# One copy of ScalarE moved ahead of two squares, and the centring of an image's first channels moved from VectorE to GpSimd

## The reference, cut to what matters

```python
x = x + dct2(group_norm(x))            # x is (16, 32, 112, 112), a 2-D cosine transform of each channel
y = group_norm(x)
for k in range(6):                     # six Euler steps of an ODE
    h = relu(gn1(y)); h = conv3x3(h, w1, t=k/6) + b1
    h = relu(gn2(h)); h = conv3x3(h, w2, t=k/6) + b2
    y = y + gn3(h) / 6
return x + y
```

## Time and the profile before

| | |
|---|---|
| median of 3 runs | 3459.21 us (3457.57 to 3469.12) |
| the profiled execution, its own time | 3467.75 us |
| span of its profile | 3465.9 us |
| mean granted TensorE clock | 0.935 |
| busy: PE / DVE / ACT / POOL | 3005.5 / 2717.9 / 2440.3 / 875.2 us |

### The profile page before, as it was taken

One profiled execution on the slowest core, in us unless ns is written; L12 is line 12 of the kernel. 1 busy time (PEld: TensorE's weight loads), 2 busy tenths in 40 slices (PEclk: granted clock), 3 DMA queues, 4 the chain that ended last, 5 costly groups with the idle time before them and its releaser, 6 DMA issues.

```text
span 3465.9 us, 148163 instructions
## 1 busy us (share of the span) xinstructions
PE 3005.5 (87%) x61684; PEld 2541.5 (73%) x61684; DVE 2717.9 (78%) x6273; ACT 2440.3 (70%) x3819; POOL 875.2 (25%) x1293
## 2 busy tenths in 40 slices
PE   3699988999889998899988999899988999888984
PEld 2578776777777787678767877777777777777873
DVE  6688876888868887788877888688886888768883
ACT  0377777677776777777776777777777767787774
POOL 3134311432123221223212331133311332111111
PEclk8799998999999999899999999999998999999997
DMA  3400033112231330322304213221133113131014
GB/s 84 89 22 22 25 55 96 49 49 80 37 96 49 91 72 4 96 77 69 68 18 112 66 49 68 59 87 49 50 67 96 49 49 92 25 95 59 31 49 112
DMA packets 370208, 217.56 MB, mean 63 GB/s; under 512 B 354544, under 2 KB 354912, under 8 KB 367456
## 3 DMA queue, kind: packets, MB, share of 16 engines
q1 hardware_dynamic: 369504, 207.64, 24.2%
HBM read 104.85 MB, written 77.07 MB: 52 GB/s over the span
## 4 chain that ended last, share of the span: by engine, by line
ACT 23%; PE 23%; issue 20%; DVE 20%; POOL 6%; DMA 3%; SPq 3%; DVEq 1%; POOLq 0%; ACTq 0%
PE cps L1482 16%; ACT z L714 8%; ACT z L682 6%; DVE y L1118 3%; PE sps L1597 3%; POOL m L562 3%; ACT unread_z L702 3%; PE tps L1588 3%; SPq L449 2%; DVE ha L1114 2%; DVE bnt L1144 2%; ACT hb L713 2%; ACT ha L713 2%; DVE hb L1114 2%; DMA y<-xa 2%
## 5 line engine op out<-in xcount | busy, mean ns | idle before, releaser
L1482 PE MATMUL cps<-ha,w 64*64 64x392 f16 (+1 forms) x27648 | 1418.8, 347 | 126.3 <-ACT z L682 75.4
L1482 PEld LDWEIGHTS cps<-ha,w 64*64 64x64 f16 x27648 | 1081.1, 110 | 332.0 <-issue 159.0
L1482 PE MATMUL cps<-hb,w 64*64 64x392 f16 x27648 | 1278.5, 334 | 20.8 <-issue 14.1
L1482 PEld LDWEIGHTS cps<-hb,w 64*64 64x64 f16 x27648 | 1091.7, 108 | 114.3 <-issue 25.9
L682 ACT ACTIVATE z<-cps,bias_now 128x784 f32<-128x784 f32 (+2 forms) x1056 | 759.1, 737 | 582.3 <-PE cps L1482 578.4
L519 POOL TENSOR_TENSOR small<-small,half 128x1 f32<-128x1 f32 x304 | 168.1, 553 | 1646.0 <-DVE small L1018 1008.4
L1114 DVE TENSOR_TENSOR ha<-z,ha 128x784 f16<-128x784 f32 (+2 forms) x384 | 385.0, 1003 | 150.4 <-ACT z L714 145.6
L1114 DVE TENSOR_TENSOR hb<-z,hb 128x784 f16<-128x784 f32 (+2 forms) x384 | 374.8, 976 | 86.6 <-ACT z L714 77.8
L1144 DVE BATCH_NORM_STATS2 bnt<-z 128x6 f32<-128x392 f32 (+1 forms) x768 | 385.8, 547 | 56.1 <-ACT z L682 55.7
L1118 DVE SCALAR_TENSOR_TENSOR y<-z,small,y 128x784 f32<-128x784 f32 (+2 forms) x384 | 396.4, 1035 | 0.1
L714 ACT ACTIVATE z<-z,small 128x784 f32<-128x784 f32 (+2 forms) x384 | 396.1, 1031 | 0.0
(11 more groups left out here) (161 smaller groups left out, 2650.9 us busy)
## 6 DMA issues: line engine op xcount, KB each, us to landing
xa<-x_dram SPq DMA_DIRECT2D x128, 196.0 KB, 5.1
y<-xa SPq DMA_DIRECT2D x16, 1568.0 KB, 7.6
y_dram<-y SPq DMA_DIRECT2D x128, 196.0 KB, 4.7
x_dram<-x1s SPq DMA_DIRECT2D x30, 784.0 KB, 6.0
fin<-y_dram SPq DMA_DIRECT2D x30, 784.0 KB, 7.5
xs<-in_x_dram SPq DMA_DIRECT2D x116, 196.0 KB, 4.5
fin<-x_dram SPq DMA_DIRECT2D x28, 784.0 KB, 5.7
out_dram<-fin SPq DMA_DIRECT2D x28, 784.0 KB, 3.6
```

The costliest lines, as they stand in the source:

```text
L1482: return pe.matmul(dst, w[hin * 64:(hin + 1) * 64, kx, a, wl, :], src[:, :, 0:NA], start=(what == "X" and n == 0), stop=(what == "Y" and n ...
```

## The change

On ACT the copy of batch 0 moves from behind the squares 2 and 3 of the second image, and behind the last part of the first image's new state, to a place ahead of the two squares. Centring of batch 0 leaves DVE and goes to GpSimd; GpSimd now centres batches 0 and 1 ahead of the first image's seam, and batch 2 behind it.

```diff
@@ GpSimd, normalise(n, b)
                 for c in range(4 * b, 4 * b + 4):
                     last = nc.gpsimd.tensor_scalar(xn[:, c, :], xs[:, c, :], m0[:, 4, c:c + 1],
                                                    m0[:, 6, CQ + c:CQ + c + 1], ALU.mult, ALU.add)
+                if b == 0:
+                    last.then_inc(xn_first, 1)
+                    pool.wait_ge(xn_first, n - HALVES + 1)
+                    return
                 last.then_inc(xn_done, 1)
@@ GpSimd, step
                 if kind == MID:
+                    normalise(HALVES * (g + 1) + s, 0)
                     normalise(HALVES * (g + 1) + s, 1)
+                seam(0, conv_at(g, s, 3), fixes + 2, pows)
+                if kind == MID:
                     normalise(HALVES * (g + 1) + s, 2)
-                seam(0, conv_at(g, s, 3), fixes + 2, pows)
                 pows = rsqrt_of(Z2, 1)
@@ ScalarE, step
+                def copied(b):
+                    if kind == MID:
+                        batch_copy(b, NBATCH * hn + b, tps)
+
...
                 evacuate(1, 1, s, 2, 3, c)
+                copied(0)
                 squares(1, 2, c, sq + 6)
                 squares(1, 3, c, sq + 7)
...
-                def copied(b):
-                    if kind == MID:
-                        batch_copy(b, NBATCH * hn + b, tps)
-
-                copied(0)
                 copied(1)
@@ VectorE
-            def normalise_first(n):
-
-                dve.wait_ge(s_nb, n - HALVES + 1)
-                for c in range(4):
-                    last = nc.vector.tensor_scalar(xn[:, c, :], xs[:, c, :], m0[:, 4, c:c + 1],
-                                                   m0[:, 6, CQ + c:CQ + c + 1], ALU.mult, ALU.add)
-                last.then_inc(xn_first, 1)
-
...
                 split_for(3, 1)
-                if kind == MID:
-                    normalise_first(hn)
                 products_of(2, 0)
```

## The result

| | before | changed |
|---|---|---|
| median | 3459.44 us (4 runs, 3457.57 to 3469.12) | 3377.37 us (4 runs, 3374.16 to 3378.36) |
| the profiled execution, its own time | 3467.75 us | 3377.95 us |

The ratio is 0.976, 95% interval 0.9744 to 0.9775: 82 us faster by the medians. The forecast was 3374 us.

What follows compares the result with a forecast made beforehand. Bound: TensorE's wait for ScalarE's copy of batch 0 and the low clock behind it. Gaining 87.3 us gives 3380.5 from the profiled 3467.75, or 3371.9 from the median; forecast 3374, range 3356 to 3419.

Steps and rivals of the forecast that it cites:

- The wait of 2.40 us and the clock behind it: TensorE before batch 1's rows: waiting for ScalarE's copy goes, 66.2 us in 28 times; 1.2 GHz level cost 1.6 or 3.1.
- The hand-over to VectorE's chain: Before the second image's activation: VectorE's statistics reading to scale and bias ends at 1118.5, TensorE's chain 0.3 earlier.
- the small losses: Before the second image's activation: 0.1 us for late VectorE and 0.1 for batch 2 beside its products, 0.2 together.
- The sum: Stretches from rows 0 to the second image's activation: 28 x 10.95 = 306.6 us instead of 393.9, a gain of 87.3.
- the split beside batch 2: GpSimd's batch 2 running beside VectorE's work: 0.1 us a step, estimated between nothing and one tenth of each product.
- VectorE's lateness: VectorE's next split starts 2.28 us behind the activation, where VectorE was free after 2.41: some 0.1 us late.
- Profile against median: Profiled execution, 8.5 us above the median: 3380 if its excess goes too, 3371.9 if it lies elsewhere; leaned to the latter.
- the seam stays where it is: GpSimd: batches 0 and 1 replace 1 and 2 ahead of the first image's seam, whose time doesn't move.
- 1.2 us to spare: GpSimd: batch 2 behind the seam takes 4.26 us, ends at 1113.9, and the second image's square root is wanted at 1115.1.
- the rival of a late GpSimd: Batch 2's centrings wait for VectorE's products, the square root comes 2.6 us late: 73 us lost, 3447; chance 0.05.
- the rival's 1.6 us a fall: TensorE's clock falls all the same from idleness before columns 0 and 2: 28 x 1.6 = 45 us lost, 3419; chance 0.10.
- the clock would hold: TensorE idles up to 1.5 us before columns 2, yet stays at full clock, as after 1.04 before the change.

Runs made afterwards that it cites:

- early split: Changed kernel with VectorE reading the second image's statistics before its last split, which fills the wait for GpSimd's square root; 3355.86 us, ratio 0.9687.
- the copy between the Relus: Changed kernel with ScalarE's copy of batch 0 behind both squares and the first of the first image's last two Relus; 3404.46 us, ratio 0.983.

## Why the prediction was right, step by step

- The wait of 2.40 us and the clock behind it: right. Both are gone in all 28 steps; moving the copy alone takes them away, moving the centring alone leaves them.
- The hand-over to VectorE's chain: right in mechanism. The early split shows it: reading ahead of the split makes the stretch 0.4 shorter. Without the small losses the chain ends at 1118.5, 10.73 us behind rows 0, and with the copy alone the step that answers to it took 10.73 (1071.47 to 1082.20). The 0.69 of idleness before columns 0, where I had 1.0, changed nothing, since PE's chain was not the last.
- The sum: 306.6 expected, 306.75 measured, and that it agrees so closely is luck. (From 1107.77 to 1118.7 are 10.93 and not 10.95, so the terms give 306.0.) I had 0.1 for the split beside batch 2; it lost 0.12. The other 0.1, for VectorE's lateness, I counted into the time to the activation, where it isn't; in its place the window begins 0.13 earlier in this step, which I hadn't seen.
- VectorE's lateness: it came out behind the activation and was larger. ScalarE waits 0.27 for VectorE's update of the state at 1086.78, and rows 3 come 9.36 instead of 9.15 behind the activation, 7.2 us over the 28 steps (263.5 for 256.3). This is the term that was mis-sized: the profiled execution's 28 first parts and the 28 windows behind them together gave 87.1 - 7.2 = 79.9. It belongs to the copy more than to the centring: with the copy alone the windows behind sum to 261.9.
- Profile against median: the profiled execution fell from 3467.75 to 3377.95, by 89.8, the median by 82. What the profile of before had above its median went, but not all of that in these steps: the first rows 0 come at 201.73 instead of 205.96, in the set-up that nobody touched. In the traces of all these kernels that point lies anywhere from 200.7 to 209.1. So 3374 came within 4 us of the median in part by luck.
- GpSimd: the step "the seam stays where it is", with 4.26 us for a batch and "1.2 us to spare", failed. Batches 0 and 1 ahead of the seam are as many instructions as before, but VectorE's own centring had been what let GpSimd through: the last two centrings of the second group took 1.23 and 0.51 beside it in the trace of the copy alone, and 1.95 and 2.63 without it in the changed kernel. It cost little: the root was still in time by 0.36, so the rival of a late GpSimd did not come about. The early split shows how near it was.
- The clock: the rival's 1.6 us a fall was measured in the copy between the Relus. That the clock would hold at 1.37 us of idleness before columns 2 was right, but I had only the 1.04 of before for it, in 7 steps the wait was even 1.51 to 1.54, and 1.53 in another place makes it fall in 8 of 28 steps. That it held was in part luck, and the chance of 0.10 was too small for what I knew.

## What to carry to other kernels

When a short copy that frees a buffer for TensorE stands behind long work on an in-order engine, the wait's own length is the lesser part of the price: look at the granted clock of the stretch behind it. After such a wait is gone, ask which chain ends last next, and whether work in front of its first instruction could fill a wait further along. Counting instructions ahead of a point on GpSimd isn't enough; what VectorE does meanwhile sets how long they take.

## What the runs showed of the hardware

GpSimd's four centrings of one batch took 2.28 us beside a VectorE that mostly waited, 4.26 with VectorE's own centrings in between, and 7.10 beside splits, updates and products alone, which all but one short cast read two tensors in SBUF. A single one of them took 2.63 us against 0.43 undisturbed, in these rows of the changed kernel:

```profile
1073.54 2.63 POOL L575 TENSOR_SCALAR xn<-xs,m 112x112 f32<-112x112 f32 x1
```

```profile
1078.31 0.43 POOL L575 TENSOR_SCALAR xn<-xs,m 112x112 f32<-112x112 f32 x1 [0.21 <-POOL ha L553]
```

The Trainium skill (SBUF — State Buffer, on the port pair that VectorE and GpSimd share) says that when an instruction of VectorE reads two tensors in SBUF and one of GpSimd reads there too, whichever starts first holds the pair for the whole instruction and the other waits. The trace agrees that GpSimd waits; but 2.63 - 0.43 = 2.2 us is a wait over more than two of VectorE's instructions of 0.96 to 1.0, and how long it can last the page doesn't state. I had read the 4.26 as the worst case because VectorE was busy throughout; busy with what was the question.

TensorE's clock: with 2.4 us of idleness before rows 1, 21 of 28 stretches were partly at 1.2 GHz, with 1.53 us there 8 of 28, with 0.7 us none. Waits of 1.51 to 1.54 us before columns 2, 7 in the changed kernel, were all followed by full clock.
